# Second loop of a graph kernel: 16-bit node parts times float16 counts, other key layout, squares on ACT, gathers without a stop

## What is computed

```python
h = relu(layernorm(x))
x = x + attention(h, edges)          # 8 heads, softmax over the edges into a node
h = relu(layernorm(x))
h = logmap0(h) @ W.T + b
msg = h[src] * (dinv[src] * dinv[dst])[:, None]     # dinv = degree ** -0.5
out = segment_sum(msg, dst)
x = x + expmap0(out)                 # expmap0(v) = tanh(|v|) / |v| * v
```

## Time and profile before

| | us |
|---|---|
| median of 3 runs | 1115.34 |
| lowest, highest | 1112.57, 1123.81 |
| span of the profiled execution | 938.0 |
| PE, DVE, ACT, POOL busy in it | 824.9, 695.7, 537.9, 588.5 |

### The profile page before, as it was taken

One profiled execution on the slowest core, in us unless ns is written; L12 is line 12 of the kernel. 1 busy time (PEld: TensorE's weight loads), 2 busy tenths in 40 slices (PEclk: granted clock), 3 DMA queues, 4 the chain that ended last, 5 costly groups with the idle time before them and its releaser, 6 DMA issues.

```text
span 938.0 us, 21433 instructions
## 1 busy us (share of the span) xinstructions
PE 824.9 (88%) x5435; PEld 625.1 (67%) x5435; DVE 695.7 (74%) x2543; ACT 537.9 (57%) x1360; POOL 588.5 (63%) x597
## 2 busy tenths in 40 slices
PE   5559988999999999999999999976599889989983
PEld 3236766767777777777677677764487677868673
DVE  8827745777777776787777777778988878888752
ACT  4486634566666666666665666607765455555530
POOL 0177755667777777777677777700466666666662
PEclk9868977999999999999999999997799999999997
DMA  6653445554544444444444444420422222222221
GB/s 175 208 137 90 115 105 95 113 126 117 128 123 118 136 113 119 131 117 120 128 113 126 128 115 133 120 77 19 107 58 60 65 53 70 56 67 59 64 60 28
DMA packets 103595, 95.99 MB, mean 102 GB/s; under 512 B 35964, under 2 KB 87393, under 8 KB 103553
## 3 DMA queue, kind: packets, MB, share of 16 engines
q0 software_dynamic: 25600, 66.10, 26.2%
q1 hardware_dynamic: 77961, 29.51, 12.7%
HBM read 84.40 MB, written 11.15 MB: 102 GB/s over the span
## 4 chain that ended last, share of the span: by engine, by line
PE 59%; POOL 14%; issue 9%; DMA 7%; DVE 5%; ACT 4%; SPq 2%; POOLq 0%; DVEq 0%
POOL kv L851 14%; PE ps_s L1815 13%; PE ps_q L1838 11%; PE ps_r L1857 10%; PE ps_f L1892 5%; DMA kv<-hs_tab,idx 4%; PE ps_c L1807 4%; PE ps_s L1825 4%; ACT ST L1608 3%; PE ps_f L1916 1%; PE ps_f L1915 1%; PE ps_c L1803 1%; PE ps_r L2017 1%; DMA qwin<-q_tab 1%; PE ps_c L1865 1%
## 5 line engine op out<-in xcount | busy, mean ns | idle before, releaser
L812 POOL DMA_INDIRECT kv<-kv_tab,idx x416 | 418.0, 1005 | 192.3 <-issue 125.3
L851 POOL DMA_INDIRECT kv<-hs_tab,idx x176 | 170.3, 967 | 141.0 <-DMA hs_tab<-qkv 54.4
L1608 ACT ACTIVATE ST<-ps_s,imj 128x512 f32<-128x512 f32 (+1 forms) x128 | 77.1, 602 | 150.1 <-PE ps_s L1825 150.0
L1815 PE MATMUL ps_s<-rep_hi,iota_b 128*128 128x512 bf16 x506 | 139.3, 393 | 0.0
L1838 PE MATMUL ps_q<-qwin,ST 128*128 128x128 f32 x832 | 128.6, 296 | 9.5 <-DMA qwin<-q_tab 6.0
L1838 PEld LDWEIGHTS ps_q<-qwin,ST 128*128 128x128 f32 x832 | 111.2, 201 | 24.8 <-issue 20.5
L1591 ACT ACTIVATE S<-iota,nloc 128x128 f32<-128x128 f32 x384 | 122.0, 389 | 0.0
L1080 DVE TENSOR_TENSOR prod<-kv,ps_q 128x512 f32<-128x512 f32 (+1 forms) x128 | 71.6, 575 | 62.7 <-PE ps_q L1838 60.4
L1857 PE MATMUL ps_r<-wv,S 128*128 128x137 f32 x832 | 111.1, 286 | 0.0
L1857 PEld LDWEIGHTS ps_r<-wv,S 128*128 128x128 f32 x832 | 103.4, 192 | 7.7 <-issue 6.8
L2017 PE MATMUL ps_r<-qkv,xt 128*128 128x128 f32 x800 | 92.0, 276 | 0.8 <-ACT xt L1733 0.8
(11 more groups left out here) (278 smaller groups left out, 1382.1 us busy)
## 6 DMA issues: line engine op xcount, KB each, us to landing
kv<-kv_tab,idx POOLq DMA_INDIRECT x416, 2.8
attr_s<-in_attr SPq DMA_DIRECT2D x32, 192.0 KB
kv<-hs_tab,idx POOLq DMA_INDIRECT x176
kv_tab<-qkv SPq DMA_DIRECT2D x4, 640.0 KB, 3.4
x_tab<-x SPq DMA_DIRECT2D x32, 64.5 KB, 2.3
qwin<-q_tab SPq DMA_DIRECT2D x32, 64.0 KB
xwin<-in_x SPq DMA_DIRECT2D x32, 64.0 KB
xwin<-x_tab SPq DMA_DIRECT2D x32, 64.0 KB
```

Source lines behind the costliest of these rows:

```text
L812: pool.indirect_dma_start(out=kv[:, b, t, :], out_offset=None, in_=kv_tab, in_offset=bass.IndirectOffsetOnAxis(ap=idx[:, b, t:t + 1], axis ...
L851: pool.indirect_dma_start(out=kv[:, j, t, 0:D], out_offset=None, in_=hs_tab, in_offset=bass.IndirectOffsetOnAxis(ap=idx[:, j, t:t + 1], ax ...
L1608: A.activation(ST[:, b, t0:t1, :], row_index(c), ACT.Abs, bias=imj[:, 0:1], scale=-1.0).then_inc(s_sta, 1)
L1815: M.matmul(ps_s[1][:], iota_b[:], busy_cols, start=True, stop=True)
```

## The change

- `hs_t` is split into three bf16 parts whose sum is exact (`hs3`, 128 x 25 x 3 x 128): ACT takes the first part in 5 passes, DVE what is left of it, ACT the second part, DVE the third. `counts` becomes float16. TensorE's counted sum is 25 matmuls of 384 columns, and DVE adds the three parts when it reads them from PSUM.
- The key is row first (row x 25 + block instead of block x 32 + row). Each tile has its own window, 14 to 34 rows wide, 400 in all instead of 15 x 32 = 480. The operands of `count` are then one run of columns each; there are 32 matmuls instead of 38. ACT's bank copies read PSUM in the old order, now with a step of 25.
- ACT squares R with dinv as its scale and gives the sum (`square`), once before and once amid its work of a pair; DVE waits for it (`s_ss1`) ahead of the root. `zz` is gone; dinv is multiplied into the last factor.
- POOL issues the 11 gathers of a pair without the wait at the seventh.
- The one-hots of pair 1 come after the third parts and the shifts; ACT copies the first counts before it builds pair 1's one-hots. Some tiles share memory in another way, 13 memsets of one column are added, and the checks of the row windows follow the new widths.

```diff
@@ -93,28 +93,33 @@
...
 NB = 5
-N1 = 17
+N1 = 14
 DG = GROUPS // 2
-W = 32
 T1 = T + 2
...
 CH2 = [(0, 4), (4, 8), (8, T2)]
-HALF2 = 6
-
-ROW0 = [min(max(round((t + 0.5) * P * N / E - W / 2), 0), P - W) for t in range(T1)]
-EB = 512 // NT
-ROWS = ROW0[-1] + W
-CB = -(-ROWS // EB)
-BANK_ROWS = [(max(ROWS - EB * (CB - k), 0), ROWS - EB * (CB - k - 1)) for k in range(CB)]
-COVER = [min(t for t in range(T1) if ROW0[t] <= e0 and ROW0[t] + W >= e1) for e0, e1 in BANK_ROWS]
-TOUCH = [[t for t in range(T1) if ROW0[t] < e1 and ROW0[t] + W > e0] for e0, e1 in BANK_ROWS]
+PARTS = 3
+
+
+ROWS_OF = [(0, 14), (4, 22), (9, 31), (16, 38), (22, 46), (30, 56), (37, 63), (43, 71), (51, 79), (58, 88), (65, 95),
+           (72, 104), (79, 111), (86, 120), (94, 128)]
+ROW0 = [lo for lo, hi in ROWS_OF]
+WIDE = [hi - lo for lo, hi in ROWS_OF]
+WMAX = max(WIDE)
+BANK_EDGES = [0, 14, 31, 51, 71, 91, 111, P]
+BANK_ROWS = list(zip(BANK_EDGES, BANK_EDGES[1:]))
+CB = len(BANK_ROWS)
+COVER = [min(t for t in range(T1) if ROWS_OF[t][0] <= e0 and ROWS_OF[t][1] >= e1) for e0, e1 in BANK_ROWS]
+TOUCH = [[t for t in range(T1) if ROWS_OF[t][0] < e1 and ROWS_OF[t][1] > e0] for e0, e1 in BANK_ROWS]
 COUNT_ORDER = [sorted([(k, t) for k in range(CB) for t in TOUCH[k] if max(t, COVER[k]) == now],
...
 FINISHED = [k for now in COUNT_ORDER for k, t in now if t == LAST[k]]
-assert FINISHED == list(range(CB))
+assert FINISHED == list(range(CB)) and max(hi - lo for lo, hi in BANK_ROWS) * NT <= 512
+assert WIDE[T:] == [WMAX] * MORE
 FREED = [1 + max(k for k in range(CB) if t in TOUCH[k]) for t in range(T1)]
+FIRST_KEYS = max(t for t in range(T1) if sum(WIDE[:t]) * NT <= 2 * T * P * 2)
 ROUND = 12582912.0
...
@@ -203,8 +208,8 @@
...
         part_rows = sb("part_rows", [2 * GROUPS, P], BF16)
-        line = sb("line", [H, 2 * GROUPS, P], BF16)
-        dloc_rows = sb("dloc_rows", [DQ, TILES // DQ, P], BF16)
+        hs3 = sb("hs3", [P, NT, PARTS, D], BF16)
+        line = hs3[0:H].rearrange("p n k d -> p (n k d)")[:, 0:2 * GROUPS * P].rearrange("p (g e) -> p g e", e=P)
         dloc_g = sb("dloc_g", [GROUPS, T, P], BF16)
...
@@ -217,8 +222,9 @@
...
         xt = sb("xt", [P, NT, D + 1])
-        xn = sb("xn", [P, XB, D])
-        hT = sb("hT", [P, 2, 4 * D])
+        xh = sb("xh", [P, 2, XB * D])
+        xn = xh[:, 0, :].rearrange("p (i d) -> p i d", d=D)
+        hT = xh[:, 1, :].rearrange("p (a e) -> p a e", a=2)
         st6 = sb("st6", [P, NT, 6])
...
@@ -272,6 +278,7 @@
...
         y_out = sb("y_out", [P, 2, D])
+        dloc_rows = y_out[:].rearrange("p b d -> p (b d)").bitcast(BF16)[0:DQ, :].rearrange("p (c e) -> p c e", e=P)
         hs_t = qkv[:].rearrange("p a c d -> p (a c d)")[:, 0:NT * D].rearrange("p (n d) -> p n d", d=D)
...
@@ -305,21 +313,21 @@
...
         src_key = runs(place(late, 1))
-        iota_key = place(late, 2, NT * W // 2).bitcast(F16)
+        iota_key = place(late, 2, NT * WMAX // 2).bitcast(F16)
         sm2 = sb("sm2", [P, 4, 2])
...
         th2 = sb("th2", [P, 2])
-        zz = prod[:, 0, 0:2, :]
         oh_keys = [ST[:].rearrange("p a t e -> p (a t e)").bitcast(BF16),
...
         def oh_key(t):
-            at = t % 8 * NT * W
-            return oh_keys[t // 8][:, at:at + NT * W]
+            at = NT * (sum(WIDE[:t]) if t < FIRST_KEYS else sum(WIDE[FIRST_KEYS:t]))
+            return oh_keys[t >= FIRST_KEYS][:, at:at + NT * WIDE[t]]
         oh_node = wv[:].rearrange("p t c -> p (t c)").bitcast(BF16)[:, 0:T1 * P].rearrange("p (t k) -> p t k", t=T1)
-        counts = xt[:, :, 0:D]
+        counts = xh[:].rearrange("p a e -> p (a e)").bitcast(F16)[:, 0:NT * P].rearrange("p (n e) -> p n e", n=NT)
+        left = xt[:, :, 0:D]
         b1d = ST[:].rearrange("p a t e -> p (a t e)")[:, 0:NT * D].rearrange("p (n d) -> p n d", d=D)
...
@@ -508,7 +519,8 @@
...
         qkv_banks = [ps_q[0], ps_q[1], ps_r, ps_c]
-        sums = [ps_r[:, 0:D], ps_f[:, D:2 * D]]
+        parts = ps_r[:, 0:PARTS * D]
+        sums = [ps_r[:, 0:D], ps_f[:, 3 * D:4 * D]]
         count_banks = [ps_f, ps_q[0], ps_q[1], ps_s[0], ps_s[1], ps_b, ps_c]
...
@@ -520,7 +532,7 @@
...
             w = BANK_ROWS[k][1] - BANK_ROWS[k][0]
-            return count_banks[k][:, 0:NT * w].rearrange("p (h e) -> p h e", e=w)
+            return count_banks[k][:, 0:NT * w].rearrange("p (e h) -> p h e", h=NT)
...
@@ -846,8 +862,6 @@
...
                 for t in range(T2):
-                    if t == HALF2:
-                        wait_apart(pool, s_g1[j], 8 * T2 * (n - j) + 16 * t, (s_pool0, 1))
                     pool.indirect_dma_start(out=kv[:, j, t, 0:D], out_offset=None, in_=hs_tab,
...
@@ -1367,7 +1382,7 @@
...
                                                op0=ALU.mult, op1=ALU.add))
-                M_.then(V.scalar_tensor_tensor(out=src_key, in0=src_key, scalar=float(W), in1=run_row[:],
+                M_.then(V.scalar_tensor_tensor(out=src_key, in0=run_row[:], scalar=float(NT), in1=src_key,
                                                op0=ALU.mult, op1=ALU.add))
...
@@ -1469,8 +1483,8 @@
...
             V.memset(R[:, 1, :], 0.0).then_inc(s_R1, 1)
-            for k in range(0, NT * W, P):
-                w = min(P, NT * W - k)
+            for k in range(0, NT * WMAX, P):
+                w = min(P, NT * WMAX - k)
                 M_.mark(V.tensor_scalar(iota_key[:, k:k + w], iota[:, 0:w], float(k), None, ALU.add))
...
@@ -1484,56 +1498,78 @@
...
                     dve.wait_ge(s_cnt, CB * (n - 1) + FREED[t])
-                V.tensor_scalar(oh_key(t), iota_key, run_col(src_key, n, t), None, ALU.is_equal).then_inc(s_ohr, 1)
+                V.tensor_scalar(oh_key(t), iota_key[:, 0:NT * WIDE[t]], run_col(src_key, n, t), None, ALU.is_equal).then_inc(s_ohr, 1)
                 V.tensor_scalar(oh_node[:, t, :], iota_b[:], run_col(src_lane, n, t), None, ALU.is_equal).then_inc(s_ohr, 1)
...
-            def window(g, b, i, st, more):
+            def chunk(c):
+                return slice(PCH * c, PCH * c + PCH)
+
+            def without_first(c):
+
+                dve.wait_ge(s_hi, c + 1)
+                V.tensor_tensor(left[:, chunk(c), :], hs_t[:, chunk(c), :], hs3[:, chunk(c), 0, :], ALU.subtract).then_inc(s_left, 1)
+
+            def third_part(c):
+
+                dve.wait_ge(s_mid, c + 1)
+                V.tensor_tensor(hs3[:, chunk(c), 2, :], left[:, chunk(c), :], hs3[:, chunk(c), 1, :], ALU.subtract).then_inc(s_hs3, 1)
+
+            def window(g, b, more):
                 dve.wait_ge(s_agg1, g + 1)
-                V.tensor_copy(R[:, b, 0:D], sums[b]).then_inc(s_R1, 1)
-                dve.wait_ge(s_R1, g + 2)
-                dve.wait_ge(s_xw1[i], 32 * ((g - i) // 4 + 1) if known(g) else (g + (4 - i)) * 8)
-                st.then(V.tensor_scalar(zz[:, b, :], R[:, b, 0:D], xwin[:, i, D:D + 1], None, ALU.mult))
+                if not (known(g) and g < 2):
+                    dve.wait_ge(s_y1, g - 1)
+                if b == 0:
+                    V.tensor_reduce(R[:, b, 0:D], parts.rearrange("p (k d) -> p d k", k=PARTS), AX_X, ALU.add).then_inc(s_R1, 1)
+                else:
+                    V.tensor_copy(R[:, b, 0:D], sums[b]).then_inc(s_R1, 1)
                 if more:
                     shift1(g + 2, b)
-                st.mark(V.scalar_tensor_tensor(out=hsq[:, b, :], in0=zz[:, b, :], scalar=1.0, in1=zz[:, b, :], op0=ALU.mult,
-                                               op1=ALU.mult, accum_out=ss2[:, b:b + 1]))
...
                 st = Steps(nc, dve, s_d1, N1 * n)
-                window(2 * n, 0, 2 * j, st, more)
+                window(2 * n, 0, more)
                 if far:
...
                     set_rest(n + 2, j)
-                window(2 * n + 1, 1, 2 * j + 1, st, more)
+                window(2 * n + 1, 1, more)
                 v_, y_, t_, a_ = [sm2[:, i, :] for i in range(4)]
-                st.sync()
+                dve.wait_ge(s_ss1, 2 * n + 2)
                 st.then(V.tensor_scalar(v_, ss2[:], 1e-30, None, ALU.max))
...
                 st.then(V.scalar_tensor_tensor(out=a_, in0=y_, scalar=1e15, in1=th2[:], op0=ALU.min, op1=ALU.mult))
+                for i in (2 * j, 2 * j + 1):
+                    dve.wait_ge(s_xw1[i], rows_in(2 * n + i - 2 * j, i))
+                st.then(V.tensor_tensor(a_, a_, xwin[:, 2 * j:2 * j + 2, D], ALU.mult))
+                dve.wait_ge(s_R1, 2 * n + 3)
                 for b in range(2):
...
                         dve.wait_ge(s_yst, 16 * (g - 1))
-                    V.scalar_tensor_tensor(out=y_out[:, b, :], in0=zz[:, b, :], scalar=a_[:, b:b + 1],
+                    V.scalar_tensor_tensor(out=y_out[:, b, :], in0=R[:, b, 0:D], scalar=a_[:, b:b + 1],
                                            in1=xwin[:, 2 * j + b, 0:D], op0=ALU.mult, op1=ALU.add).then_inc(s_y1, 1)
...
             with dve.If_eq(in_order, 1):
-                for n in range(2):
-                    for t in range(T1):
-                        run_one_hots(n, t)
+                for c in range(NT // PCH):
```

(50 more changed lines are left out.)

22 lines of the change are left out of this document (14 added, 8 removed).

## The result

The kernel after takes 1164.4 us, median of 4 runs (1157.88 to 1174.58), against 1113.95 for the kernel before in the same comparison: the ratio on record is 1.051, 95% interval 1.045 to 1.057 (the two medians alone make 1.045). It is slower; 1084 was predicted, with 1079 to 1101 as the range.

The account below looks back on a forecast made before the run. POOL's gathers were taken to bound the second loop. 34 us from removing the stop, less 2 for the lead-in and 0.3 for the tail, rounded down to 31: 1115.3 - 31 = 1084 us, range 1079 to 1101.

Parts of the forecast that it names:

- the first term of the sum: Second loop, POOL: without the wait at the seventh gather a pair takes 13.95 us instead of 16.10, 34 us in all.
- Nothing else holds POOL in steady state: Second loop: waits before a pair's first gather, for indices and earlier sums, add nothing to the usual 0.30 us idle.
- the nearest row for an unbroken run: First loop's gathers, without a wait on a landing, taken as model: 1.005 + 0.30 us each, upper bound 14.36 a pair.
- Counted sums: TensorE, L2017: 25 matmuls of 384 16-bit columns take 4.64 us instead of 5.75, a gain of 1.1.
- copies of 500 values: ACT's seven stepped PSUM copies writing float16: taken as unchanged at 0.59 us each, at most doubled.
- turns of TensorE: TensorE's busy time a second-loop pair: 14.37 us before the change, 12.3 after, below POOL's 13.95.
- The lead-in: Before the second loop's early pairs: DVE 7.0 us longer, pair 2's indices at 693.9; charged 2 us, between 0 and 5.
- The tail: From the last landing to the end, 13.9 us: square on ACT and product replace scaling and square, +0.3 us.
- DVE as the bound: Rival, chance 0.20: odd-half key rows at half rate bring DVE to 14.6 us a pair, past POOL; time 1098.
- POOL locked out by DVE's one-hots: Second loop: each gather waits out one key one-hot, 18.6 us a pair, +38 us, 1153; chance 0.01 of the 0.06.
- The stop's wait comes back: Rival, chance 0.08: a filling queue holds POOL at the gather itself; only 0 to 5 us won, 1110 to 1115.
- TensorE's clock stays low: Rival, chance 0.06: at 1.2 GHz throughout, PE's turn is 24.6 us a pair, 128 us slower, about 1243.

Follow-up runs that it names:

- paced: Without the stop, two small POOL writes ahead of every second second-loop gather: kernel after 0.993 (1092, again 1094 us), kernel before 0.996 (1098 us), each against the kernel before.

## Why the prediction was wrong
**The step that failed** is the first term of the sum, "Without it a pair is 11 gathers x (0.966 mean + 0.30) = 13.93". The gathers do step at 1.27 without the stop, and 2 us go from POOL's turn. What the sum lacked is that at this pace the gathers take the other engines' time: from the fifth on, PE, DVE and ACT fall from some 12 instructions a us to about 2, for 9 to 10 us, until some 2 us after the last. "Nothing else holds POOL in steady state" then ends: it waits 7 to 10 us for indices from a VectorE that stood. Taken out alone, the stop does not win 34 us: the kernel is some 100 us slower.

**Where the trace misled.** The first loop in the profile shown, "the nearest row for an unbroken run", has runs like these without a stall. But its span of 938.0 stood against times of 1112 to 1124, and I wrote "I leave that distance as it is". This distance was no overhead around the span (2 us in all later runs): the profile was of an execution without what makes up the rest. The second loop there has free runs too. From 804.83 on, five gathers of one pair and six of the next follow each other at 1.25 to 1.34, and the engines go on (columns as in the earlier trace rows):

```profile
804.83:811.26 6.43, 6.27 (x44) 3.71 (x42) 4.29 (x19) 3.85 (x9) 4.90 (x6) 1.00 0.32 82
811.26:820.87 9.61, 8.38 (x75) 8.38 (x76) 8.54 (x41) 5.03 (x16) 5.83 (x7) 1.00 0.19 48
```

PE, DVE and ACT start 72 instructions in 6.4 us and then 132 in 9.6, 11 and 14 a us. So a free run of gathers does not by itself make a stall: it did in the later executions and not in this one of the same kernel. What else it takes is open.

**The other terms.** The sizes were near. Counted sums: 4.64 forecast, 4.5 to 4.8 in the blocks at mostly full clock (872.74: 4.77; 1006.49: 4.47). Reduction 0.55 (0.43 to 0.6), square 0.40 and its read 0.19 (0.39 to 0.59), copies of 500 values 0.60 to 0.66 (taken as unchanged from 0.59), product 0.16. All of this together was worth nothing where POOL sets the pair: paced, the two kernels are equal. With the stop the kernel after is 1.012 of the kernel before; its runs across the pair's border stall. With neither stop nor pause it counts: 24.5 us a pair in the kernel before, 21.5 in the kernel after, and 3.0 x 15 = 45 us is near what lies between 1211 and 1164. In the two pairs shown the kernel before has no longer stall than the kernel after (9.09 against 10.03), but a longer stretch behind it (9.28 against 6.27), and there TensorE is busy nearly throughout, at clocks of 0.71 and 0.62. The forecast's turns of TensorE, 14.4 and 12.3, give 2.1 of the 3.0; the rest is not accounted for. So the result can be read as some +100 us from the stop and -47 from the rest. That split holds for this order alone: taken the other way round, the rest costs 1.2 per cent with the stop in, and the stop's removal then 3.8.

The lead-in was charged 2 us, 5 at most; pairs 0 and 1 took 18.2 + 16.8 = 35.0 instead of 27.9, 7 us. Of these some 2.5 are the wait that was charged (pair 2's first gather has 2.83 idle before it, not 0.30); most of the others are longer gathers in pair 0, one of 3.50. The tail was to grow by 0.3; from the last gather's start to the end it is 22.0 (1133.70 to 1155.7) instead of 15.6 (1097.73 to 1113.3), since the last run of gathers stalls the others too.

**The rivals.** DVE as the bound: no. The 650- and 550-column rows, whose halves are odd counts, take 0.393 and 0.378; the 600 and 700 beside them, with even halves, 0.377 and 0.403. No key row loses its rate. The Trainium skill, VectorE: DVE Perf Modes, section Mode 2×_1P, asks for 4-byte alignment, which the odd halves break; the Trainium skill, Vector Engine (DVE) Microarchitecture Reference, section 5.1, says that this makes no difference, and with that the trace agrees. POOL locked out by DVE's one-hots: hardly. Gathers beside which a key row runs for more than 0.3 us take 0.99 in the mean (22 of them between 860 and 1120), gathers without any 0.94 (102), and a key row takes 0.34 to 0.45; the steps stay at 1.24 to 1.36. The Trainium skill, SBUF — State Buffer, section Who interferes with whom, has DVE block POOL for a whole instruction; the trace shows no wait of that length. "The stop's wait comes back" had a queue that fills at the gather itself: the gathers keep 0.94. It does come back, ahead of the pair's first gather and four times as long, through VectorE. "TensorE's clock stays low" had the sign (0.06) and the mark that I named, a clock well below 1.00 (0.80 over the second loop). But the clock stood at 1.00 when the stall began, and VectorE and ScalarE stood with TensorE while each of their instructions kept its length (0.26 and 0.39 on VectorE and 0.66 on ScalarE, the means of their lines); the low clock follows the stall and adds to it.

## What stays open
By what means a run of gathers stops the other engines' sequencers is not shown. It is not the bytes moved (half of them change nothing) and not the lack of a drain (two gathers always under way at a slower step do little harm). The rate is not told apart from the number of gathers under way at once, which goes with it. The Trainium skill, NOTIFIC — the notification-queue block, section 7.1, says that the block which writes the engines' event records holds its producers back inside rather than lose one. No run here shows whether that is at work: every execution of the experiments was recorded with its span and clock, so the kernel without such records is not among them.

## What to carry over
Before costing anything, hold the profile's span against the times: if they differ by more than the few us around a launch, the profile is of another execution than the one you want to make faster. A wait that looks like dead time on one engine may be what lets the others run, so price its removal on the engines beside it, by an experiment that takes it out alone. Where indirect gathers follow each other and such stalls show, try to pace them: here a pause of 0.6 us ahead of every second gather did at least as well as a stop of 2 us for landings.

## What was not expected of the hardware
- Gathers at a step of 1.26 us bring PE, DVE and ACT together from 11 to 13 instructions a us down to 1.6 or 2.4 after the fifth; at 1.37 there are stalls still, at 1.26 and 1.84 in turn hardly any. One execution of the kernel before ran eleven at 1.25 to 1.34 without a stall.
- A gather of 64 rows costs POOL 0.90, one of 128 rows 0.94: the price is almost all fixed.
- One write of 2 columns between two gathers costs nothing (0.12 in a gap of 0.30); a second one, waiting for the first, costs 0.58.
